# Projections and first attention of the first layer in one block, without the barrier between them

## The reference

```python
x = x + _L0_xattn_ref(_layernorm(x, axis=-1), ctx_4096, ctx_4096, L0_xattn_Wq, ..., L0_xattn_bo)
x = x + _L0_ffn_ref(_layernorm(x, axis=-1), L0_ffn_weight, ..., L0_ffn_gb2)

def _L0_xattn_ref(query, key, value, Wq, bq, Wk, bk, Wv, bv, Wo, bo):
    EMBED = 512; NUM_Q = 32; NUM_KV = 8; GROUPS = 4; HEAD_DIM = 16; KV_DIM = 128
    Q = query @ Wq + bq;  K = key @ Wk + bk;  V = value @ Wv + bv
    ...
    scores = jnp.einsum('bhgqd,bhkd->bhgqk', Q, K) * scale
    w = jax.nn.softmax(scores, axis=-1)
    y = jnp.einsum('bhgqk,bhkd->bhgqd', w, V)
    y = y.transpose(0, 3, 1, 2, 4).reshape(B, S, EMBED)
    return y @ Wo + bo
```

## Time and profile before

| | us |
|---|---|
| runs | 1726.32, 1727.17, 1729.74 |
| median | 1727.17 |
| profiled execution, its own time | 1734.99 |
| span in its profile | 1733.3 |
| share of the span: PE, PEld, DVE, ACT, POOL | 92%, 77%, 65%, 45%, 60% |

### The profile page before, as it was taken

How to read it: one execution, slowest core, us unless ns; L and a number is a source line. 1 busy time by engine, 2 the same in 40 slices (tenths; PEclk the granted TensorE clock), 3 DMA queues, 4 the chain that set the end, 5 groups by cost and what they waited for, 6 DMA issues and landing times. The chain is left out here.

```text
span 1733.3 us, 26194 instructions
## 1 busy us (share of the span) xinstructions
PE 1593.3 (92%) x8546; PEld 1341.8 (77%) x8546; DVE 1119.0 (65%) x2271; ACT 786.5 (45%) x2552; POOL 1032.7 (60%) x1074
## 2 busy tenths in 40 slices
PE   6499975699999999999999999999999999996896
PEld 5377863588888888888888788888888888885784
DVE  4277866377767677678787555576655555554684
ACT  4297842244444444344444344444544544443342
POOL 6544421367767787767675666566756776553452
PEclk9799996699999999999999999999999999998895
DMA  6632100322222222212221222222222332211000
GB/s 209 164 69 47 44 1 1 91 62 74 68 74 72 75 81 72 62 56 69 69 65 54 74 68 68 60 75 67 74 67 75 85 98 81 67 56 47 16 25 25
DMA packets 73702, 117.20 MB, mean 68 GB/s; under 512 B 9632, under 2 KB 21280, under 8 KB 73568
## 3 DMA queue, kind: packets, MB, share of 16 engines
q1 hardware_dynamic: 73344, 115.26, 23.5%
q10 hardware_dynamic: 224, 0.26, 0.0%
HBM read 108.15 MB, written 7.34 MB: 67 GB/s over the span
## 5 line engine op out<-in xcount | busy, mean ns | idle before, releaser
L1200 POOL TENSOR_TENSOR a_probs<-a_probs,a_total 128x512 f32<-128x512 f32 x128 | 133.2, 1041 | 249.3 <-DVE a_total L1632 247.7
L47 PE MATMUL ps<-a_wo_hi,a_oT_lo 128*128 128x512 f32 x512 | 212.3, 415 | 1.6 <-DVE a_oT_lo L1648 1.6
L49 PE MATMUL ps<-a_wo_hi,a_oT_hi 128*128 128x512 f32 x512 | 201.5, 394 | 0.0
L1471 ACT ACTIVATE a_probs<-a_cross,a_neg_max 128x128 f32<-128x128 f32 x512 | 198.2, 393 | 4.1 <-DVE a_neg_max L1624 2.1
L48 PE MATMUL ps<-a_wo_lo,a_oT_hi 128*128 128x512 f32 x512 | 199.9, 390 | 0.0
L62 POOL TENSOR_TENSOR a_wo_lo<-k_ring,a_wo_hi 128x512 fp32r<-128x512 f32 x128 | 165.6, 1294 | 10.2
L62 POOL TENSOR_TENSOR a_w_lo<-k_ring,a_w_hi 128x512 fp32r<-128x512 f32 x126 | 162.9, 1293 | 10.1
L62 DVE TENSOR_TENSOR a_pT_lo<-ps,a_pT_hi 128x512 fp32r<-128x512 f32 x194 | 129.7, 682 | 18.9 <-ACT a_pT_hi L1482 8.9
L1618 DVE TENSOR_TENSOR a_cross<-ps,a_cross 128x512 f32<-128x512 f32 x128 | 87.8, 686 | 68.9 <-ACT a_cross L1465 66.5
L1216 POOL TENSOR_TENSOR a_scales<-a_scales,neg_half 128x5 f32<-128x5 f32 x64 | 74.8, 1168 | 95.5 <-DVE a_scales L1585 95.2
L1455 ACT ACTIVATE a_kT<-ps,k_weight 128x128 fp32r<-128x128 f32 x64 | 23.5, 368 | 207.1 <-PE ps L1270 207.1
(11 more groups left out here) (411 smaller groups left out, 4989.9 us busy)
## 6 DMA issues: line engine op xcount, KB each, us to landing
k_ring<-in_L_wq SPq DMA_DIRECT2D x132, 256.0 KB, 2.6
k_ring<-in_L_wo SPq DMA_DIRECT2D x128, 256.0 KB, 2.6
k_ring<-in_L_wkv SPq DMA_DIRECT2D x66, 256.0 KB, 2.6
h_q_stack<-q_part SPq DMA_DIRECT2D x24, 256.0 KB, 4.5
k_ring<-in_L_main SPq DMA_DIRECT2D x12, 256.0 KB, 3.1
p_c_raw<-in_cT SPq DMA_DIRECT2D x4, 512.0 KB, 6.2
x<-in_x SPq DMA_DIRECT2D x8, 256.0 KB, 7.9
q_part<-p_part_hi SPq DMA_DIRECT2D x8, 256.0 KB, 2.7
```

The source lines that it names most:

```text
L47: pe.matmul(out, lhs_lo, rhs_hi, start=start, stop=False)
L49: return pe.matmul(out, lhs_hi, rhs_hi, start=False, stop=stop)
L1200: pool.tensor_tensor(heads(probs[:, :]), heads(probs[:, :]), along_last(total[:, :], S), ALU.mult).then_inc(s["probs"], 1)
L1471: act.activation(head(probs, h), head(cross, h), ACT.Exp, bias=neg_max[:, h:h + 1], scale=1.0 if normed(t) else SCALE, accum_out=total[:, ...
```

## The change

Both parts of layer 0 now stand in one block. The engine programs are Python generators: at a `yield` of the projections the next item of the attention's list is emitted, so that each engine's list is projections with some attention items between them. The barrier and its waits are gone; waits on the semaphores of the first part (`before[...]`) stand where the attention takes over a resource. Tiles are shared by hand (`Shared`): the weights' tiles become `pT`, `oT` and `xT`, parts of `c_raw` become `probs`, and the small gate tiles lie in the tile of the parts. One memory clearing scope with its barrier at the end of layer 0 goes too (two all-engine barriers stood there, one stands there now).

```diff
+        def bank_of(c, h):
+            n = number[c, h]
+            return banks[n % 4 if n < 8 else n - 4]
...
             for n in range(SETS):
                 save(Q_CHUNK + n, 1)
-                if n in (0, 2):
-                    load_late(4 + n // 2)
+                if n == 0:
+                    load_late(4)
             held.load_stacks(sp, 1, s["stacked1"])
-            for p in (0, 1):
-                sp.wait_ge(s[f"saved{p}"], 160)
-                sp.wait_ge(s[f"stacked{p}"], 16 * STACK_LOADS)
+            load_late(5)
...
-            for k in range(len(late)):
-                ...
+            for k in range(4):
+                if k < 3:
+                    split_late(k)
+                for b in (2 * k, 2 * k + 1):
+                    pool.wait_ge(s["xn"], b + 1)
+                    pool.tensor_tensor(x_of(b), x_of(b), bo_row[:, :], ALU.add).then_inc(s["biased"], 1)
+            yield
+            yield
+            yield
+            for k in range(3, len(late)):
+                split_late(k)
+                yield
...
-                elif n >= 8:
-                    pe.wait_ge(s["part_lo"], n - 5)
+                elif n >= 10:
+                    pe.wait_ge(s["v_taken"], 2)
...
             for n in range(SETS):
                 product(Q_CHUNK + n, 1)
+                if n in (1, 2):
+                    yield
...
             for n in range(SETS):
                 round_part(Q_CHUNK + n, 1)
+                if n == 1:
+                    yield
...
             for n in range(SETS):
                 low_part(Q_CHUNK + n, 1)
+                if n == 1:
+                    yield
+                    yield
...
+        def one_after_the_other(first, second):
+            for _ in first:
+                next(second)
+            for _ in second:
+                pass
...
+            def place_values(i):
...
+                if i < 2:
+                    pool.wait_ge(before["mm"], 12)
+                    for x in v_s[i]:
+                        pool.memset(x.bitcast(F32), 0.0).then_inc(s["zeroed"], 1)
+                    pool.wait_ge(s["zeroed"], 2 * (i + 1))
...
+                    if turn == 0:
+                        place_values(0)
...
                 if kind == "score":
-                    if r == 0 and i >= 2:
+                    if turn < 2:
+                        pe.wait_ge(before["part_lo"], 4 + 2 * turn)
+                    if r == 0 and i < 2:
+                        pe.wait_ge(before[f"stacked{i}"], 16 * STACK_LOADS)
+                    elif r == 0:
                         pe.wait_ge(s["stacked"], 16 * STACK_LOADS * (i - 1))
```

More of the change, by code:

```diff
@@ L88, in sems, with late_sems @@
         return {n: self.sem(n) for n in names.split()}
+    def late_sems(self, names):
+        return {n: self.sem("late_" + n) for n in names.split()}
 def tiles_of(bank):
@@ new lines, in heads_and_gates @@
+        pT = [tuple(x[:, blk(p, RW)] for x in (w_hi, w_lo)) for p in (0, 1)]
+        oT, xT = (tuple(x[:, blk(k, D)] for x in (w_hi, w_lo)) for k in (4, 5))
+        raw_max, neg_max = ([shared.stats[:, (2 * n + p + 1) * RH:(2 * n + p + 2) * RH] for p in (0, 1)] for n in (0, 1))
+        total = [shared.moments[:, blk(p, RH)] for p in (0, 1)]
+        xn, products = shared.bo[:, 0:D], shared.c_raw[:, blk(1, B * S)]
+        kept = shared.parts[:, 0:B * SIDE0].bitcast(F32)
+        small = shared.small
@@ new lines, in heads_and_gates @@
+        stats, moments, rstd = small(6), small(2), small(1)
+        routed, rT = probs[0], pT[0]
+        widths = (GATE_HID,) * 3 + (E * GATE_HID, E)
+        b1, gamma, beta, w2, b2 = rows = [
+            shared.c_raw[:, 2 * B * S + sum(widths[:k]):2 * B * S + sum(widths[:k + 1])] for k in range(5)]
+        row_sources = [A[n] for n in ("L0_ffn_gb1", "L0_ffn_ln_gamma", "L0_ffn_ln_beta", "L0_gw2", "L0_ffn_gb2")]
+        hid, dev = small(HALF_B * GATE_HID), small(HALF_B * GATE_HID)
+        stat, inv = small(HALF_B), small(HALF_B)
@@ L521, in heads_and_gates @@
+        gates, first, second, rest = (small(B * E) for _ in range(4))
+        best, following, rank, share, ratio = (small(B) for _ in range(5))
+        counts, allowed = small(2 * E), small(2 * E)
+        next_stats, next_moments, next_rstd, next_shift = (small(w * B) for w in (6, 2, 1, 1))
         next_xn = [xn, probs[1][:, 0:D]]
-        s = ph.sems("stacked rows zeroed v_hi v_lo s_mm raw_max neg_max exped inverse probs pT_mm pT_hi pT_lo av_mm oT_hi oT_lo"
+        s = ph.late_sems("stacked rows zeroed v_hi v_lo s_mm raw_max neg_max exped inverse probs pT_mm pT_hi pT_lo av_mm oT_hi oT_lo"
@@ L699, in _ @@
                     act.wait_ge(s["side"], i + 1)
+                    if i == 0:
+                        for p in (0, 1):
+                            act.wait_ge(before[f"saved{p}"], 160)
                     act.activation(kept[:, blk(i, SIDE0)], bank_x[:, 0:SIDE0], ACT.Copy).then_inc(s["kept"], 1)
+                yield
             act.wait_ge(s["ahead"], 1)
@@ L808, in _ @@
                     dve.wait_ge(s["added"], i + 1)
+                    if i == 0:
+                        dve.wait_ge(before["biased"], B)
+                        for p in (0, 1):
+                            dve.wait_ge(before[f"saved{p}"], 160)
                     dve.bn_stats(stats[:, :], x_of(i)).then_inc(s["stats"], 1)
```

167 lines of the change are left out of this document (89 added, 78 removed).

## The result

The changed kernel takes 1718.01 us (median of 4 runs, 1717.40 to 1718.62), the kernel before took 1728.45 us beside it (4 runs, 1726.32 to 1730.77). The ratio is 0.9936, 95% interval 0.9923 to 0.9948: **faster by 10.4 us, 0.64%**. Forecast were 1719.2 us and 8.0 us of gain from the old median. The profiled execution of the changed kernel took 1717.59 us, its span is 1715.9 us; for these the forecast was 1727.0 and 1725.3, which is 9.4 too much.

The account below looks back on a forecast made before the run. PE's 17.1 us wait for the barrier between the two blocks was the loss, afterwards POOL would bind; 8.3 + 0.3 - 0.6 = 8.0 us gained, 1727.2 - 8.0 = 1719.2 us, range 1715.5 to 1723.5 (8 in 10).

Parts of the forecast that it names:

- POOL's turn 0 starts: Start of POOL's first attention multiplication in layer 0: at 69.9 us and not at 83.58, 13.7 us earlier.
- mark: First scores of sequence 2 on PE, followed to read the gain: at 98.5 us and not 106.81, 8.3 earlier.
- second barrier at the exit: End of layer 0: two passages through a barrier become one, 0.3 us gained.
- The handoff between DVE and POOL: DVE's small operations meeting POOL's instructions on the shared port, turns 0 to 4: 1.0 us for POOL, between 0 and 1.7.
- The tail: From the start of POOL's turn 4 multiplication to the first scores of sequence 2: 7.2 us, before 8.0.
- My 0.6 us for it: Loss to low clock from PE's pauses between 69 and 92 us: a fifth of one spell, between 0 and 4.
- Rival (b): Steady part after 92 us loses one or two low-clock spells of 3.3 us: gain 3.5 to 6, some 1722; chance 0.22.
- POOL is the bound of these five turns: Turns 0 to 4 of layer 0's attention: POOL's queue of multiplications, splits and placings takes 20.4 us with no pause left.
- rival (a): POOL does not bind, the whole 13.7 us are kept: 1713.2 us; chance 0.13 together with a middle case of 1716.4.
- The interleaving: Attention items between the last projections: PE waits 4.4 us at the stacks, Q2 takes 5.1, Q3 ends at 68.0.
- Rival (d): Scores start no earlier than the products allow, interleaving costs what it brings: within 3 us of before, 1725.5; chance 0.07.
- Rival (c): Slower: SP's load of `up` waits for the split of `main`, delaying sequence 2's stacks; at 101 it is 1730.7; chance 0.03.

Follow-up runs that it names:

- clean `xn`: Kernel before plus twelve already fulfilled waits on DVE, where it waits for the first attention turn's exponentials; all eight `xn` short; 1727.32 us against 1729.11, ratio 0.9992.

## Why the prediction was right, and where its sizes were off

The sign, the time and the chain held. The time fits better than the gain (off by 1.2 us against 2.4), and that much is luck: the kernel before took 1728.45 us beside the changed one, 1.3 more than the median that the forecast started from. Step by step:

| step | forecast | measured |
|---|---|---|
| first scores start, PE's wait there | 58.5, 4.4 | 57.76, 4.03 |
| Q2 at the low clock | 5.1 | 4.8 (58.75 to 63.55) |
| POOL's turn 0 starts | 69.9 | 68.68 |
| turn 0 to turn 4 on POOL | 20.4 + 1.0 | 20.69 |
| turn 4 to the mark | 7.2 | 6.77 |
| mark | 98.5 | 96.14 |
| stacks of sequence 1 | landed by 79.8, cost 0 | in time for 79.49, cost 0 |
| SP at the load of `up` | near 80 | issued 78.57 |
| second barrier at the exit | 0.3 gained | not seen |
| gain in the medians | 8.0 | 10.4 |

**The mark** came 2.4 us earlier than forecast, and three terms share it. The start of turn 0 gave 1.2: everything upstream ran some 0.4 earlier, and the stacks landed earlier than I rounded. The clock fell at 56.3 us, 2.6 after PE stopped; I had read 3.9 from the rows, so the half microsecond "to spare" was no measure. The handoff between DVE and POOL gave 0.7: I priced it at 1.0 for POOL and it cost 0.3, of which 0.21 is the one pause. The tail gave 0.4. POOL was hardly ever the one that waited. DVE was held for up to 2.67 us, and this cost at most that pause, since the ring waited for POOL. I had put the longest hold at the 1.90 of one multiplication; this one began in turn 0's multiplication and lasted over both zeroings behind it. In the changed kernel repeated, the tail took 7.66 us instead of 6.77, with a mean clock of 0.79 where the first profile has 1.00, after the same pause of 2.10 us of PE. The two stretches:

```profile
89.00:97.00 8.00, 5.25 (x33) 4.14 (x33) 4.53 (x10) 5.91 (x27) 4.86 (x4) 1.00 0.38 85
```
```profile
88.00:96.00 8.00, 5.37 (x28) 4.77 (x29) 4.56 (x10) 5.91 (x26) 4.85 (x4) 0.79 0.42 89
```

So this term is no constant: it differed by 0.9 us between two executions of one kernel. My 0.6 us for it lies between the two (0 and 0.9). Rival (b), one or two spells more in the steady part, did not come: from 96 to 216 us the clock is 1.00 in both. The next low spell of the first profile (216.8 to 220.2) has a longer counterpart in the kernel before (230.8 to 237.6). The sum in that rival was off: two spells of 3.3 us leave 2.0 us of gain and not 3.5, some 1725, outside my range.

**"POOL is the bound of these five turns"** was true by 1.0 us only. I had named it in bold from the sum of its queue alone, without adding up the ring beside it at the low clock. This did no harm to the forecast and would have misled the next step: whoever frees POOL by 5.7 us gets 1.0, and behind it stand the stacks of sequence 1. In rival (a) I also had POOL's old pauses wrong: between the two multiplications they add up to 6.8 us (0.90 + 2.97 + 1.87 + 1.10) and not 5.7, which changes nothing in the argument.

**The interleaving** carried half of my working (the wait at the stacks, the slow Q2, Q3's end at 68.0), and it is neutral. Rival (d) said that it costs what it brings, and that is so; but it concluded from this that the change brings little, and that does not follow, since POOL starts at 68.2 to 68.7 either way.

**Rival (c)** was the right place with the wrong form. The load of `up` can indeed take the gain, as it did when it stood ahead of the stacks of sequence 1. With the load in its new place there were 8 us to spare: the stacks of sequence 2 were issued from 78.97 to 84.13, landed by about 88 (3.7 us later), and were needed at 96.14.

**The second barrier** gave nothing: with clean `xn` the kernel before takes 197.75 us from mark to exit, and the changed kernel 197.84 and 197.66.

**What I had not seen** is the late `xn`. I read its pause in the rows and used it as a price for the clock, not as a loss that the change could move. I wrote that spells of low clock behind the mark would show me wrong if they were new, and did not ask whether an old one would vanish. It did, and this explains 4.4 of the 17.4 us between the profiled executions; 10.7 are the mark, and the rest, some 2, lies behind, where no late `xn` stands. The kernel before's own median lies below its profiled execution by 6.5 us. I counted the gain at the mark, ahead of that place, and took it to the median unchanged. That came out; whether the mark moves alike in executions without a profile was not measured. Taking the difference of the two profiles for the gain would have been wrong by 7 us.

## What to carry to other kernels

When a barrier goes, follow each queue that stood behind it: here one DMA that waits for a slow engine, left ahead of the loads that the next stage needs, gives back most of the gain. Before an engine is called the bound, add up the ring beside it as well; what lies between the two sums is all that freeing the engine can bring. And when two profiles differ by more than the medians, profile the old kernel a second time before the difference is explained.

## What the runs showed of the hardware that was not expected

- An instruction of DVE with nothing to wait for starts 0.23 to 0.28 us late at places 128 apart in its stream. It is not seen at every such place (the kernel before has none at its 320th instruction); that longer instructions ahead hide it is an inference. It costs where POOL's next instruction is ready at the same moment: 0.24 us late became 1.5 us more on `xn`, and PE's pause grew from 0.55 to 2.4 us.
- An inverse sum of 128x8 numbers, 0.20 us elsewhere, took 1.87 us beside POOL's zeroings, and a negative maximum ahead of it 2.67. Both ended with a zeroing (71.41 + 0.96 = 72.37 us). Whether the inverse sum was held itself or only stood behind the negative maximum was not separated.
- The same kernel has the clock at 1.00 in one execution and at 0.79 in another, over the 8 us around the same place, after the same pause of 2.10 us.
